# Seam of a decoder layer: first M and V·Wo loaded in eight pieces each over the last rounds, split inside rounds, scores first in two tiles

## What is computed

```python
x = x + self_attention(layernorm(x))               # 16 heads of 32, causal, output projection
x = x + cross_attention(layernorm(x), ctx, ...)    # 16 query heads of 128, 8 kv heads, 64 keys per batch
x = x + ffn(layernorm(x))                          # 8 experts, the best one for each token, rank 64
```

## Time and profile before

| | us |
|---|---|
| median of 3 runs | 1533.86 |
| lowest and highest | 1533.47, 1535.66 |
| the profiled execution | 1535.35 |
| its span, first to last instruction | 1533.6 |
| PE busy in it | 1382.5 (90%) |
| DVE, ACT, POOL busy | 1092.7, 729.9, 757.2 |
| mean granted TensorE clock | 0.966 of full |

### The profile page before, as it was taken

How to read it: one execution, slowest core, us unless ns; L and a number is a source line. 1 busy time by engine, 2 the same in 40 slices (tenths; PEclk the granted TensorE clock), 3 DMA queues, 4 the chain that set the end, 5 groups by cost and what they waited for, 6 DMA issues and landing times.

```text
span 1533.6 us, 28325 instructions
## 1 busy us (share of the span) xinstructions
PE 1382.5 (90%) x10592; PEld 1140.9 (74%) x10592; DVE 1092.7 (71%) x2037; ACT 729.9 (48%) x1739; POOL 757.2 (49%) x570
## 2 busy tenths in 40 slices
PE   7878778999998999999995778999999999999998
PEld 5656667777787877777874567888888887888886
DVE  4336486777878787877775577878787877787865
ACT  5444567666676667676674432323232323232221
POOL 2321266767777676867675643334343433343310
PEclk9999989999999999999998789999999999999999
DMA  8999587879898979888888731313130313030000
GB/s 321 306 316 292 118 153 135 166 159 160 169 162 160 164 141 182 162 168 168 155 145 232 189 144 47 116 34 125 30 138 28 133 33 132 28 136 30 28 15 28
DMA packets 378872, 212.57 MB, mean 139 GB/s; under 512 B 337648, under 2 KB 337776, under 8 KB 375024
## 3 DMA queue, kind: packets, MB, share of 16 engines
q1 hardware_dynamic: 378736, 210.74, 57.1%
HBM read 76.49 MB, written 50.33 MB: 83 GB/s over the span
## 4 chain that ended last, share of the span: by engine, by line
PE 48%; DVE 26%; issue 5%; ACT 4%; DMA 4%; POOL 2%; SPq 0%; DVEq 0%; ACTq 0%; POOLq 0%
PE banks L44 35%; DVE a_neg_max L803 4%; PE banks L936 4%; PE banks L1535 3%; DMA a_turned<-shared 3%; DVE b_xn L1378 2%; PE banks L970 2%; DVE a_y_sum L822 2%; DVE shared L812 2%; ACT a_probs L706 2%; PE banks L944 2%; DVE b_probs L1427 1%; PE banks L971 1%; DVE b_row_sum L1432 1%; DVE b_row_max L1425 1%
## 5 line engine op out<-in xcount | busy, mean ns | idle before, releaser
L626 POOL TENSOR_TENSOR shared<-a_probs,shared 128x768 f16<-128x768 f32 (+1 forms) x192 | 349.4, 1820 | 204.9 <-DVE shared L812 183.0
L706 ACT ACTIVATE a_probs<-banks,a_neg_max 128x128 f32<-128x128 f32 (+3 forms) x512 | 265.1, 531 | 210.9 <-DVE a_neg_max L803 184.0
L803 DVE TENSOR_REDUCE a_neg_max<-banks 128x2 f32<-128x256 f32 (+3 forms) x256 | 203.7, 818 | 115.4 <-PE banks L944 114.7
L1231 POOL TENSOR_TENSOR b_probs<-b_probs,b_row_scale 128x1024 f32<-128x1024 f32 x32 | 61.0, 1907 | 200.8 <-DVE b_row_scale L1437 200.8
L970 PE MATMUL banks<-a_v,a_turned 128*128 128x96 bf16 x1280 | 123.5, 212 | 32.3 <-DMA a_turned<-shared 25.8
L970 PEld LDWEIGHTS banks<-a_v,a_turned 128*128 128x128 f16 x1280 | 99.8, 100 | 65.5 <-issue 34.5
L1212 POOL TENSOR_TENSOR b_rstd<-b_var,b_minus_half 128x1 f32<-128x1 f32 x64 | 35.3, 551 | 189.4 <-DVE b_var L1373 189.4
L1304 ACT ACTIVATE b_probs<-b_probs 128x1024 f32<-128x1024 f32 x32 | 33.9, 1059 | 182.2 <-DVE b_probs L1427 182.2
L971 PE MATMUL banks<-a_v,a_turned 128*128 128x64 bf16 x1280 | 119.3, 196 | 0.0
L44 PE MATMUL banks<-a_xt_hi,w_qkv_hi 128*128 128x512 f32 x256 | 110.5, 432 | 6.5 <-DVE a_yt_lo L777 4.7
L706 ACT ACTIVATION_READ_ACCUMULATOR a_probs<-banks,a_neg_max 128x1 f32 x512 | 105.9, 207 | 0.0
(11 more groups left out here) (172 smaller groups left out, 3983.2 us busy)
## 6 DMA issues: line engine op xcount, KB each, us to landing
m_dram<-c_m_out SPq DMA_DIRECT2D x8, 2048.0 KB, 13.7
vw_dram<-shared SPq DMA_DIRECT2D x32, 512.0 KB, 8.3
b_vw_raw<-vw_dram SPq DMA_DIRECT2D x8, 2048.0 KB, 8.0
shared<-m_dram SPq DMA_DIRECT2D x7, 2048.0 KB, 8.4
c_w_raw<-w_group_dram SPq DMA_DIRECT2D x7, 1280.0 KB, 11.5
a_x_res<-x_dram SPq DMA_DIRECT2D x32, 256.0 KB, 3.5
x_dram<-a_x_res SPq DMA_DIRECT2D x32, 256.0 KB, 2.9
b_x<-x_dram SPq DMA_DIRECT2D x32, 256.0 KB, 2.7
```

The source lines that it names most:

```text
L626: nc.gpsimd.tensor_tensor(part(u, 1), probs[:, u % PROB_SLOTS, 0:2 * columns_of(u // 2)], part(u, 0), ALU.subtract).then_inc(parts_ready, 1)
L706: ins = nc.scalar.activation(probs[:, u % PROB_SLOTS, to:to + width], score[:, j, at:at + width], ACT.Exp, bias=neg_max[:, c:c + 1], accum ...
L803: ins = nc.vector.tensor_reduce(neg_max[:, c:c + 2], score[:, 2 * half:2 * half + 2, at:at + width], AX, ALU.max, negate=True)
L1231: nc.gpsimd.tensor_tensor(probs[:, :, :], probs[:, :, :], row_scale[:, :].unsqueeze(2).to_broadcast([P, XH, S]), ALU.mult).then_inc(probs_ ...
```

## The change

- SP loads M of batch 0 in eight 256 KB pieces, one in each of rounds 84 to 91 (`INPUTS_FREE_AT`), behind the round's transposes. Round 92 brings x1 tile 0, round 93 x1 tile 1 and the mask, rounds 94 and 95 one piece of vw each. The four `x_res` loads move from round 95 to just behind round 95's transposes, and the other six pieces of vw and x1 tiles 2 and 3 follow them. Memory is laid out anew for this (`PLACE`), and vw of batch 0 has semaphores of its own.
- ACT splits M in rounds 93 and 94, two chunks in each. POOL takes chunk 0 at the end of round 94 and chunk 2 at the end of round 95, DVE chunk 1 in round 95 and chunk 3 after it.
- The low parts of vw: DVE takes chunks 1, 2 and 3, POOL chunk 0.
- In tile 1, ACT splits the expert weights behind the exponentials and behind x2's transposed tile; POOL takes both its expert parts behind the probabilities.
- In tiles 2 and 3 PE makes the scores first (`lead`).

```diff
@@ self_attention, SP
-    LAST_X_RES_AT = B * NR - 1
+    LAST_X_RES_AT = B * NR
+        INPUTS_FREE_AT = (B - 1) * NR
...
+                if r == INPUTS_FREE_AT:
+                    sp.wait_ge(gemm_drained, drained((B - 1, "xt", KT - 1)))
+                if INPUTS_FREE_AT <= r < INPUTS_FREE_AT + XG:
+                    next(then)
                 if r == WEIGHTS_FREE_AT:
                     sp.wait_ge(gemm_full, PROJECTED)
                     sp.wait_ge(x1_stored, TT * 16)
                     sp.wait_ge(vw_stored, XG * 64 + 64)
+                if WEIGHTS_FREE_AT <= r < B * NR:
                     next(then)
+            next(then)
             for u in range(2 * B * NR - PART_SLOTS, 2 * B * NR):
                 sp.wait_ge(turned_landed[u % TURN_SLOTS], landed(u))
             next(then)
@@ POOL, ACT
-                if r == B * NR - 2:
+                if r in (B * NR - 2, B * NR - 1, B * NR):
                     next(then)
-                if r == B * NR:
-                    pool.wait_ge(parts_ready, 2 * B * NR)
-                    next(then)
-                if r == B * NR + 1:
-                    next(then)
+            pool.wait_ge(parts_ready, 2 * B * NR)
             next(then, None)
...
-            next(then)
+                if r in (B * NR - 3, B * NR - 2):
+                    next(then)
             high_part(LAST[0])
@@ cross_attention_and_experts, SP
-        for t in range(TT):
-            load_x1((0, t, t))
+        def load_m_first(g):
+            sp.dma_start(m_first[g // HALF][:, g % HALF, :], m_dram[0, :, g, :]).then_inc(m_first_loaded, 16)
+        def load_vw_first(g):
+            sp.dma_start(vw_raw[:, g * D:(g + 1) * D], vw_dram[0, :, g, :]).then_inc(vw_first_loaded, 16)
+        for g in range(XG):
+            load_m_first(g)
+            yield
+        load_x1((0, 0, 0))
+        yield
+        load_x1((0, 1, 1))
         sp.dma_start(mask_u8[:, :], mask.to_broadcast([P, B * S])).then_inc(small_loaded, 16)
-        sp.dma_start(m_first[:, :], m_dram[0].rearrange("p g m -> p (g m)")).then_inc(m_first_loaded, 16)
-        load_vw(0)
+        yield
+        load_vw_first(0)
+        yield
+        load_vw_first(1)
+        yield
+        for g in range(2, XG):
+            load_vw_first(g)
+        load_x1((0, 2, 2))
+        load_x1((0, 3, 3))
         yield
         load_m(1)
-        sp.wait_ge(vw_lo_by_pool, len(VW_POOL))
-        sp.wait_ge(vw_lo_by_dve, len(VW_DVE))
+        sp.wait_ge(vw_first_lo_ready, CHUNKS)
@@ ACT
-            if second:
-                act.wait_ge(we_loaded, 16)
-                for k in range(KT):
-                    nc.scalar.activation(we_hi[:, k, :], ...
...
+            if second:
+                act.wait_ge(we_loaded, 16)
+                for k in range(KT):
+                    nc.scalar.activation(we_hi[:, k, :], ...
+                for c in M_BESIDE[t]:
+                    split_m(b + 1, c, 1 - par)
...
-        act.wait_ge(m_first_loaded, 16)
-        for c in range(CHUNKS):
-            split_m(0, c, 0)
+        act.wait_ge(m_first_loaded, XG * 16)
+        split_m(0, 0, 0)
+        split_m(0, 1, 0)
+        yield
+        split_m(0, 2, 0)
+        split_m(0, 3, 0)
         yield
@@ DVE
+        m_low(1)
         normalise(2, x1[:, 0, :], 0)
         yield
-        m_low(1)
         m_low(3)
...
-        for c in VW_DVE:
+        for c in range(1, CHUNKS):
             vw_low(0, c)
@@ PE
+            lead = isinstance(here, int) and 1 < here < TT
+            if lead:
+                make_scores(b, t, here, par)
             if done and not second:
-                turn_probs(done[2], here is not None)
+                turn_probs(done[2], here is not None and not lead)
...
-            if here is not None and not second:
+            if here is not None and not second and not lead:
                 make_scores(b, t, here, par)
```

More of the change, by code:

```diff
@@ L1052, in cross_attention_and_experts @@
     vw_raw = at("vw_raw", PLACE["vw_raw"], [P, KT * EW], F32)
-    m_first = at("m_first", PLACE["m_first"], [P, MW], F32)
+    m_first = [at(f"m_first{n}", PLACE[f"m_first{n}"], [P, HALF, KT * 2 * S], F32) for n in range(2)]
     m_hi, m_lo = ([at(f"m{p}_{n}", PLACE[f"m{p}_{n}"], [P, MW], F32R) for p in range(2)] for n in ("hi", "lo"))
@@ L1253, in step @@
             if second:
+                we_low(0)
                 we_low(2)
@@ L1269, in gpsimd @@
         vw_low(0, 0)
-        vw_low(0, 2)
-        yield
-        vw_low(0, 3)
         deviation(2, 2)
@@ L1317, in step @@
                 copy_hi(flat(xt3_hi), turn[2][:, :], xt3_full, gated[2] + 1, xt3_hi_ready)
-            if second:
-                act.wait_ge(we_loaded, 16)
-                for k in range(KT):
-                    nc.scalar.activation(we_hi[:, k, :], vw_raw[:, expert_rows(k)], ACT.Copy).then_inc(we_hi_ready, 1)
-            if is_tile(b) and is_tile(b + 1):
+            if is_tile(b) and is_tile(b + 1) and not second:
                 for c in M_BESIDE[t]:
```

46 lines of the change are left out of this document (28 added, 18 removed).

## The result

The change makes the kernel slower. The kernel after took 1546.10 us (median of 4 runs, 1543.46 to 1547.04), the kernel before 1533.66 us beside it. The two medians are 12.4 us apart. The ratio is 1.0071, with a 95% interval from 1.0053 to 1.0089, so some 10.9 us are lost by it (8.1 to 13.6). I had said 1529.6, with a range up to 1535.5: the sign is wrong and the range misses.

What follows compares the result with a forecast made beforehand. PE was taken as busy except for three idle stretches between round 91 and tile 3. Terms -1.2 - 1.4 - 1.0 - 2.1 + 1.0 + 0.4 = -4.3 us gave 1529.6 against the median 1533.86; range 1523.5 to 1535.5.

Steps and rivals of the forecast that it cites:

- The 4 MB leave the transposes' way: Seam's start: PE's 17.20 us wait goes, the mask becomes late, issued about 831.0 and landing at 835.5, 1.5 us later.
- POOL then sets the last transpose: After the mask: POOL starts unit 187 at 840.8, needs 15.2 us, finishes unit 191 at 856.0; its transpose lands at 860.2.
- Then comes vw: Behind the last transpose: ten 256 KB loads take 8.4 us, until 868.6; tile 0's mask added at 874.2, gaining 1.2 us.
- The forecast's case: Before tile 0's mask: vw's landing is the bound, time 1527 to 1532.5, likeliest 1529.6; chance 0.47.
- PE's own scores of tile 0 are ready by then: Tile 0, when its mask is added at 874.2: PE's side of the seam runs some 7 us earlier.
- Tile 0: Tile 0: PE's waits of 0.52 us for POOL and 0.92 for DVE go, gaining 1.4 us.
- Tile 1: Tile 1: exponentials and subtraction gain 1.0 us, normalisations without POOL's expert part 2.1; experts' low parts still take 4.65.
- Scores first in tile 3: Tile 3: making scores first gains nothing at the start and bares the copies of turned probabilities, costing 1.0 us.
- The pieces in rounds 84 to 91: Rounds 84 to 91: eight 256 KB loads cost 0.4 us in all, within bounds of 0 and 6.7.
- the second: Seam: mask lands by its 6.6 us (+2.1), pieces take 10 us (+1.6), the rest gives back; 1533.3, chance 0.17.
- The third: Rounds 84 to 91: load pieces delay transposes, each round giving 0.84 us to PE; +2.0, up to 1536.5, chance 0.11.
- The fourth: Loads behind the last transpose: ten pieces at 2.7 us each land 18.6 us later than forecast; 1548, chance 0.03.

## Why the prediction was wrong

The step that failed is the end of the chain: POOL's units, vw behind them, and DVE's work of tile 1 beside POOL's. The sum went wrong in four terms. It ends at the attended product of tile 2, where it said -4.7 us and +6.4 were measured, 11.0 more (4.0 to tile 0's mask, 1.3 in tile 0, 4.4 in tile 1, 1.3 in tile 3). Behind that, where the prediction had no change, another 1.6 us come in up to the seam's end. In the table each time counts from round 93's first row maximum, 822.51 in the row that the prediction used and 825.01 after.

| step | said | measured | off by |
|---|---|---|---|
| DVE meets the mask | 13.0 | 14.2 | +1.2 |
| POOL starts unit 187 | 18.3 | 19.5 | +1.2 |
| POOL has done unit 191 | 33.5 | 37.6 | +4.1 |
| last piece of vw landed | 46.1 | 50.2 | +4.1 |
| mask added, tile 0 | 51.7 | 55.7 | +4.0 |
| mask added, tile 1 | 70.1 | 75.4 | +5.3 |
| x1 of batch 1 reaches DVE | 93.2 | 102.9 | +9.7 |
| attended product, tile 2 | 113.3 | 124.3 | +11.0 |

- **"*The 4 MB leave the transposes' way*": right as a mechanism, mis-sized.** The mask was issued at 10.6, not 8.5. Unit 185 was finished when I said (POOL's end 830.83), but SP was still held in the transpose ahead of it, unit 184's, until 832.01, and then 1.78 us more in its own. Two stores and an x1 tile had been issued just before (826.34 to 828.21), and the queue moved 219 to 256 GB/s, though no bulk load was in it. I had read the 17.03 us of the earlier trace rows as the price of the 4 MB alone, and put nothing for this. The landing took 3.6, a little less than my 4.5.
- **"*POOL then sets the last transpose*": right, and 2.8 us too short.** From unit 187 to 191 it took 18.0 us for the 15.2 that I summed. Units 190 and 191 took 2.57 and 3.12 where I put 2.13 each. When they started, DVE had an operation on SBUF of its own under way, a cast until 857.49 and a low part of M until 860.56, and each unit ended 2.0 us behind that. The small operations, with a wait of 0.49 us among them, took 1.2 us more than I gave them.
- **"*Then comes vw*": right.** From unit 191 to the last piece 12.6 us were said, 12.7 measured; from there to the mask added 5.6 and 5.5. The forecast's case, vw as the bound, is what happened. What I did not see is how far from the end of the other work it stood: PE had tile 0's scores ready at 870.8, 10 us before the mask was added to them. My line "PE's own scores of tile 0 are ready by then" should have been turned into a price, since whatever delays vw is paid in full from there.
- **Tile 0: failed (-1.4 said, -0.1 measured).** The 1.4 us of waits for POOL and DVE did go. But PE, idle for 10.23 us ahead of tile 1's scores, had fallen to the half clock, and these took 7.5 us in place of 5.7. In the kernels in which mask and vw are both early, the step takes 17.9 us in place of 19.8, with PE kept busy: the 1.4 I had said, and a little more.
- **Tile 1: half right, and the costly half wrong.** The exponentials' gain came (from the mask added to the row sums 4.85 us, before 5.93). "In tile 2, with POOL idle, they take 1.00": they took 3.19, for POOL's two expert parts now stand beside exactly these. And "still take 4.65" was 7.00. The prediction read the 4.65 as the price of two parts with POOL "on its own two at the same time". In the kernel before, POOL's low part of M stood beside the first of DVE's two, and the second ran alone: 3.45 and 1.28. In the kernel after, POOL has one operation more in that stretch, so that both of DVE's meet one: 3.61 and 3.47. The rows, before and then after:

```profile
908.26 3.45 DVE L1415 TENSOR_TENSOR b_we_lo<-b_vw_raw,b_we_hi 128x1088 fp32r<-128x1088 f32 x1
911.63 1.28 DVE L1415 TENSOR_TENSOR b_we_lo<-b_vw_raw,b_we_hi 128x1088 fp32r<-128x1088 f32 x1
...
912.36 3.61 DVE L1446 TENSOR_TENSOR b_we_lo<-b_vw_raw,b_we_hi 128x1088 fp32r<-128x1088 f32 x1
915.89 3.47 DVE L1446 TENSOR_TENSOR b_we_lo<-b_vw_raw,b_we_hi 128x1088 fp32r<-128x1088 f32 x1
```

  For the normalisations and the low parts together -2.1 was said and +2.4 measured. This is where the x1 tile gets its further 4.4 us.
- **Scores first in tile 3: right sign, size wrong.** Said +1.0; 3.2 and 3.7 us came back in the seam when it was undone, and 2.8 were lost when it was made alone. The prediction counted the bare copies. It left out that 24 score matmuls are now ahead of the turned probabilities, 8.5 us, since the first 13 run at the half clock, and that DVE adds the mask only behind the low parts of these, so that it starts this chain at 950.8, 4 us after the scores are there.
- **"*The pieces in rounds 84 to 91*": right.** Said +0.4, measured +0.3 in the mean of all profiles.

Of the rivals, the second came nearest, by its mechanism (mask and vw late), but it promised that "the rest gives back what they lose", and the rest lost as well. The third, the one that ended slower, had the wrong place (its own terms, -4.7 and +6.7, give 1535.9, where it says up to 1536.5). The fourth did not happen: the ten pieces went out from 863.96 and had all landed at 875.2, after 11.3 us, where ten times 2.7 are 27. The 2 us of fixed time that the prediction takes there from the Trainium skill (DMA: Bandwidth & Descriptors, Anatomy of one DMA) are the page's fit for DMAs that GpSimd issues; SP issues these. No rival joined the late chain with the new meetings of DVE and POOL, and so none reached 1546.

**What isn't settled.** The seam explains 7.4 to 8.0 us, the rounds ahead of it about 0.3. From the mask added to tile 4 to the end of the span it takes 574.3 to 575.5 us in the 16 kernels made from the kernel after, and 573.2 to 573.8 in the four made from the kernel before: 1.3 us more in the mean, in code whose order the change leaves alone. I didn't test why. The sum, 9.0 to 9.6, lies inside the ratio's interval (8.1 to 13.6 us). The new layout of memory was never undone alone, and neither was the early load of M.

## What to carry to other kernels

- A stall that is removed is worth only the distance to what is late next; write for each load that is moved when its user could at the earliest start, and ask what stands on that chain now. Here loads that had long landed became the last ones: 2 MB moved from ahead of the last transposes to behind them, and a mask of 64 KB moved behind a pair of transposes that held the queue's issuer for 5.57 us.
- Work that is moved off one engine's critical place lands beside other work. List, for DVE and POOL, which operations will run at the same time, and cost those at the price of a row in which the two do meet.
- A small load that everything waits for goes first, rounds ahead; bulk goes where the issuer would wait with an empty queue, in parts that fit between two transposes; a tile that is needed soon goes ahead of 2 MB. With the parts in tiles 1 to 3 undone as well, these moves gave a kernel 1.4% under the one before (1513.78 us beside 1535.20, ratio 0.9860), where the change as made costs 0.7%.
